# Mixer's step plan: two tiles a step behind each scan, and the shared expert's first unit in step 8 of 20

## The reference, cut to what matters

```python
h = layernorm(x) * (1 + ca) + sa
x_shift = (roll(h, -T//2) @ Wts.T) * sigmoid(gate) + h * (1 - sigmoid(gate))
xn = layernorm(x_shift) * ln_w + ln_b
k, v = xn @ Wk.T, xn @ Wv.T                      # 64 wide
wkv = exp(-exp(time_first) * sigmoid(k)) * v
states = scan(s * exp(time_decay) + wkv_t)       # along the tokens
x = x + ga * (states @ Wo.T)
h = layernorm(x) * (1 + cb) + sb
shared = (silu(h @ Wsg) * (h @ Wsu)) @ Wsd * sigmoid(h @ Wse)   # 1408 wide
routed = top 4 of 32 experts (352 wide, at most 64 tokens each), weights softmax(h @ Wr)
x = x + gb * (shared + routed)
```

## Time and profile before

| | us |
|---|---|
| median of 3 runs | 720.41 (719.29 to 721.12) |
| profiled execution | 720.49 |
| its span, first to last instruction | 718.70 |
| PE busy in the span | 672.3 (94%) |
| DVE / ACT / POOL busy | 367.4 / 288.9 / 185.1 |

### The profile page before, as it was taken

The page is one execution under the profiler, slowest core; times in us unless marked ns, Lnnn a source line. Parts: engine busy times, 40 slices in busy tenths (PEclk is TensorE's granted clock), DMA queues, the critical chain, the costliest instruction groups (busy, mean ns, idle before and its releaser), DMA issues.

```text
span 718.7 us, 8895 instructions
## 1 busy us (share of the span) xinstructions
PE 672.3 (94%) x3218; PEld 466.0 (65%) x3218; DVE 367.4 (51%) x714; ACT 288.9 (40%) x552; POOL 185.1 (26%) x174
## 2 busy tenths in 40 slices
PE   4798688999998899998999899999999999999997
PEld 3665455767676667886665566666666666667875
DVE  3779677678678877763214223122122243225755
ACT  3445775665656633323225124233232343323231
POOL 1254565645536200001122022222221212120000
PEclk9899978999999999999999999999999999999999
DMA  7670200001232008206777767878899787816311
GB/s 276 232 250 0 76 15 30 15 31 30 74 122 84 15 1 281 85 1 242 266 231 239 257 217 253 263 238 280 271 322 339 239 270 261 284 22 234 117 49 69
DMA packets 50295, 118.27 MB, mean 165 GB/s; under 512 B 6904, under 2 KB 11084, under 8 KB 50252
## 3 DMA queue, kind: packets, MB, share of 16 engines
q1 hardware_dynamic: 45388, 109.31, 43.0%
q0 software_dynamic: 4864, 8.40, 5.4%
HBM read 100.87 MB, written 18.91 MB: 167 GB/s over the span
## 4 chain that ended last, share of the span: by engine, by line
PE 61%; DVE 5%; DMA 3%; ACT 2%; issue 2%; POOL 2%; SPq 0%; DVEq 0%; ACTq 0%; POOLq 0%
PE bank L1686 28%; PE bank L1698 11%; PE bank L1741 11%; PE bank L1758 6%; DMA egu<-in_L_ffn_Wu_dram 2%; PE bank L1729 1%; ACT xsH L860 1%; DMA xg<-h_rows,slot_tok 1%; PE bank L1789 1%; PE bank L1747 1%; DVE xres L1260 1%; DVE prodL L1224 1%; POOL ho L634 1%; DVE prod L1222 1%; POOL xres L642 1%
## 5 line engine op out<-in xcount | busy, mean ns | idle before, releaser
L1686 PE MATMUL bank<-xsH,wguH 128*128 128x512 f32 x352 | 143.8, 408 | 1.7 <-DVE xsL L1214 1.3
L1686 PE MATMUL bank<-xsL,wguH 128*128 128x512 f32 x352 | 138.0, 392 | 0.0
L1686 PE MATMUL bank<-xsH,wguL 128*128 128x512 f32 x352 | 137.7, 391 | 0.0
L1741 PE MATMUL bank<-egu,xeT 128*64 128x352 f32 x512 | 80.9, 469 | 3.3 <-DMA egu<-in_L_ffn_Wu_dram 3.3
L1686 PEld LDWEIGHTS bank<-xsH,wguH 128*128 128x128 f32 x352 | 66.6, 189 | 26.4 <-issue 10.8
L1222 DVE TENSOR_TENSOR prod<-bank,silu 128x512 f32<-128x512 f32 x38 | 26.2, 690 | 110.7 <-PE bank L1686 87.7
L1698 PE MATMUL bank<-wdH,prodH 128*128 128x512 f32 x176 | 73.7, 419 | 6.3 <-DVE prodL L1224 4.1
L692 POOL DMA_INDIRECT expert_sums<-ye,slot_to x32 | 49.2, 1537 | 116.7 <-DMA expert_sums<-ye,slot_to 92.0
L1686 PEld LDWEIGHTS bank<-xsL,wguH 128*128 128x128 f32 x352 | 66.3, 188 | 14.7
L1686 PEld LDWEIGHTS bank<-xsH,wguL 128*128 128x128 f32 x352 | 66.6, 189 | 13.0 <-issue 0.7
L699 POOL DMA_INDIRECT xg<-h_rows,slot_tok x16 | 16.8, 1050 | 221.3 <-ACT ye L899 90.2
(11 more groups left out here) (222 smaller groups left out, 1020.8 us busy)
## 6 DMA issues: line engine op xcount, KB each, us to landing
egu<-in_L_ffn_Wg_dram SPq DMA_DIRECT2D x32, 704.0 KB, 6.2
egu<-in_L_ffn_Wu_dram SPq DMA_DIRECT2D x32, 704.0 KB, 7.7
ed<-in_L_ffn_Wd_dram SPq DMA_DIRECT2D x32, 512.0 KB, 5.2
h2T<-in_L_wmod_dram SPq DMA_DIRECT2D x6, 1024.0 KB, 8.7
ed<-in_L_ffn_Wd_dram SPq DMA_DIRECT2D x32, 192.0 KB, 6.3
h_rows<-ho SPq DMA_DIRECT2D x16, 256.0 KB, 2.0
expert_sums<-ye SPq DMA_DIRECT2D x16, 256.0 KB, 8.9
out_dram<-xres SPq DMA_DIRECT2D x16, 256.0 KB, 2.2
```

The costliest lines, as they stand in the source:

```text
L1686: ins = mm.matmul(bk[:, :], l[f][:, w, c, :], r[:, c, :], start=(k == 0), stop=(k == 3 * C - 1))
L1741: ins = mm.matmul(bk[side, 0:F], xeT[:, c, side], egu[:, e, w, c, :], start=(c == 0), stop=(c == C - 1))
```

## The change: what it does

A group's tiles no longer leave one a step, five steps behind their mixer. The new function `outs(t)` gives the tiles that step t projects: none in the step of the group's scan, two in the step behind it, two in the next, none in the fourth. The router of a group stands in that fourth step (t = 7, 11, 15, 19), the shared expert's first unit begins in step 8, and the loop ends after 20 steps. Every engine's step function uses `outs`. ho gets a fourth buffer with its own semaphore; POOL's `out_rstd` stands behind `mix_rows`; the weight splits of the first part (`split_first`, `first_lo`) stand a step earlier; SPLIT_FIRST names the last step alone, and ROUTER_FIRST and the early `lo_group` of step 17 go.

```diff
-        STEPS = NT + 6
-        FFN_FROM = 10
-        ROUTER_FIRST = (9, 17)
-
-        SPLIT_FIRST = (17, 21)
+        STEPS = NT + GT
+        FFN_FROM = 2 * GT
+
+        SPLIT_FIRST = (STEPS - 1,)
+
+        def outs(t):
+
+            g, k = divmod(t - GT, GT)
+            return range(g * GT + 2 * (k - 1), g * GT + 2 * k) if 0 <= g < NG and 0 < k < 3 else ()
...
-            if t >= 6:
-                turns.append(("h2", t - 6))
+            turns += [("h2", i) for i in outs(t - 1)]
...
-            return (t - 9) // GT if t % GT == 1 and t >= 9 else None
+            return t // GT - 1 if t % GT == GT - 1 and t >= GT else None
...
-            PRODUCTS += [("router", router_group(t))] if t in ROUTER_FIRST else []
-            PRODUCTS += [("project", t - 5)] if 0 <= t - 5 < NT else []
+            PRODUCTS += [("project", i) for i in outs(t)]
...
@@ POOL's step loop @@
-                    if 0 <= t - 5 < NT:
-                        out_rstd(t - 5)
...
                     if t + 1 < NT:
                         mix_rows(t + 1)
-                    if t >= 7:
-                        scale_sum(t - 7)
-                        h2_rows(t - 7)
+                    for i in outs(t):
+                        out_rstd(i)
+                    for i in outs(t - 2):
+                        scale_sum(i)
+                        h2_rows(i)
...
-                scale_sum(NT - 1)
-                h2_rows(NT - 1)
+                for i in outs(STEPS - 2):
+                    scale_sum(i)
+                    h2_rows(i)
...
@@ ACT's step loop @@
-                    if t in ROUTER_FIRST:
-                        logits_out(router_group(t))
-                    if 0 <= t - 5 < NT:
-                        norm_out(t - 5)
+                    for i in outs(t):
+                        norm_out(i)
...
-                    if 4 <= t < 4 + NC0 + 1:
-                        split_first(t - 4)
+                    if 3 <= t < 3 + NC0 + 1:
+                        split_first(t - 3)
...
@@ DVE's step loop @@
-                    if t == 17:
-                        lo_group(0, g + 1)
...
-                    if 0 <= t - 5 < NT:
-                        residual_sum(t - 5)
+                    for i in outs(t):
+                        residual_sum(i)
...
-                    if t >= 7:
-                        scale_rows(t - 7)
+                    for i in outs(t - 2):
+                        scale_rows(i)
...
-                scale_rows(NT - 1)
+                for i in outs(STEPS - 2):
+                    scale_rows(i)
...
@@ PE's step loop @@
-                    new_states = t == 13
-                    if 0 <= t - 5 < NT and not new_states and t not in ROUTER_FIRST:
-                        project(t - 5)
+                    new_states = t % GT == 1
+                    for i in () if new_states else outs(t):
+                        project(i)
...
                     if g >= 0:
                         early_piece(g, 2 * s)
-                    if 0 <= t - 5 < NT and new_states:
-                        project(t - 5)
+                    for i in outs(t) if new_states else ():
+                        project(i)
...
-                    if t in ROUTER_FIRST:
-                        project(t - 5)
```

More of the change, by code:

```diff
@@ L79, in build @@
     R = E + 2
+    HO = 4
     assert (H, S, C, CAP * 2, BT, NP, FS % P, HB, PARTS[0]) == (512, 64, 4, P, 8, 16, 0, GT, 2)
@@ L138, in build @@
             mx = sb("mx", [P, 3, H], F32, pa)
-            ho = sb("ho", [P, 3, H], F32, pa)
+            ho = sb("ho", [P, HO, H], F32, pa)
             kvW = sb("kvW", [P, C, P], F32, pa)
@@ L256, in build @@
          xhat_ok, hi_ok, lo_ok, wr_zero, s_full0, s_full1, s_taken0, s_taken1, mix_ok,
-         xn_ok, ho_ok, h2_ok, h2_sent0, h2_sent1, h2_sent2, e_tanh, e_fac, st_ok,
+         xn_ok, ho_ok, h2_ok, h2_sent0, h2_sent1, h2_sent2, h2_sent3, e_tanh, e_fac, st_ok,
          vef_ok, vex_ok, veh_ok, rsf_ok, rsx_ok, rsh_ok, dve_self, pool_self,
@@ L263, in build @@
              "xhat_ok hi_ok lo_ok wr_zero s_full0 s_full1 s_taken0 s_taken1 mix_ok "
-             "xn_ok ho_ok h2_ok h2_sent0 h2_sent1 h2_sent2 e_tanh e_fac st_ok "
+             "xn_ok ho_ok h2_ok h2_sent0 h2_sent1 h2_sent2 h2_sent3 e_tanh e_fac st_ok "
              "vef_ok vex_ok veh_ok rsf_ok rsx_ok rsh_ok dve_self pool_self "
@@ L281, in build @@
         stage_in = (stage_in0, stage_in1, stage_in2)
-        h2_sent = (h2_sent0, h2_sent1, h2_sent2)
+        h2_sent = (h2_sent0, h2_sent1, h2_sent2, h2_sent3)
         d_full, d_used, y_in = (d_full0, d_full1), (d_used0, d_used1), (y_in0, y_in1, y_in2, y_in3, y_in4)
@@ L348, in build @@
             PRODUCTS += [("mixer", t)] if t < NT else []
-            PRODUCTS += [("router", router_group(t))] if t in ROUTER_FIRST else []
-            PRODUCTS += [("project", t - 5)] if 0 <= t - 5 < NT else []
+            PRODUCTS += [("project", i) for i in outs(t)]
             PRODUCTS += [("kv", scan_group(t))] if scan_group(t) is not None else []
-            PRODUCTS += [("router", router_group(t))] if t not in ROUTER_FIRST and router_group(t) is not None else []
+            PRODUCTS += [("router", router_group(t))] if router_group(t) is not None else []
         turn_at, turns_in = {}, dict.fromkeys(T_BANKS, 0)
@@ L511, in _ @@
                     sp.wait_ge(h2_ok, t + 1)
-                    sp.dma_start(h2_dram[t * P:(t + 1) * P, :], ho[:, t % 3, :]).then_inc(h2_sent[t % 3], 16)
+                    sp.dma_start(h2_dram[t * P:(t + 1) * P, :], ho[:, t % HO, :]).then_inc(h2_sent[t % HO], 16)
                     if t == BT - 2:
@@ L534, in load_down @@
                         sp.dma_start(ed[0:F - 2 * P, e, 2, :], Wd[2 * j + e, 2 * P:F, :]).then_inc(dn_in, 16)
-                for k in range(3):
-                    sp.wait_ge(h2_sent[k], 16 * len(range(k, NT, 3)))
+                for k in range(HO):
+                    sp.wait_ge(h2_sent[k], 16 * len(range(k, NT, HO)))
                 sp.wait_ge(wlo_ok, splits(2, 0))
@@ L633, in h2_rows @@
                         pool.wait_ge(sb_in, 16 * (b + 1))
-                    gp.tensor_tensor(ho[:, t % 3, :], ho[:, t % 3, :], bc[:, PLACE[K_SB], :], ALU.add).then_inc(h2_ok, 1)
+                    gp.tensor_tensor(ho[:, t % HO, :], ho[:, t % HO, :], bc[:, PLACE[K_SB], :], ALU.add).then_inc(h2_ok, 1)
                 def scale_sum(t):
@@ L783, in norm_out @@
                         act.wait_ge(part_full, len(VECTORS))
-                    else:
-                        act.wait_ge(h2_sent[t % 3], 16 * (t // 3))
+                    elif t >= HO:
+                        act.wait_ge(h2_sent[t % HO], 16 * (t // HO))
                     act.wait_ge(nbh_ok, t + 1)
-                    a.activation(ho[:, t % 3, :], xres[:, t, :], ACT.Identity, scale=rsh[:, at], bias=nbh[:, at]).then_inc(hn_ok, 1)
+                    a.activation(ho[:, t % HO, :], xres[:, t, :], ACT.Identity, scale=rsh[:, at], bias=nbh[:, at]).then_inc(hn_ok, 1)
                 def part_out(n):
@@ L986, in _ @@
                     if router_group(t) is not None:
-                        if t not in ROUTER_FIRST:
-                            logits_out(router_group(t))
+                        logits_out(router_group(t))
                         sigma_exp(router_group(t))
@@ L1178, in scale_rows @@
                     turn_full(dve, ("h2", t))
-                    v.tensor_tensor(ho[:, t % 3, :], ho[:, t % 3, :], bc[:, PLACE[K_1CB], :], ALU.mult).then_inc(ho_ok, 1)
+                    v.tensor_tensor(ho[:, t % HO, :], ho[:, t % HO, :], bc[:, PLACE[K_1CB], :], ALU.mult).then_inc(ho_ok, 1)
                 def kv_scan(g):
@@ L1437, in _ @@
                             first_rows(i)
-                    if t >= 7:
-                        scale_rows(t - 7)
+                    for i in outs(t - 2):
+                        scale_rows(i)
                     if g >= 0 and s == 3:
                         top_experts(g)
-                    if 6 <= t < 6 + NC0 + 1:
-                        first_lo(t - 6)
+                    if 5 <= t < 5 + NC0 + 1:
+                        first_lo(t - 5)
                     if t == 4:
@@ L1458, in _ @@
                         derive_gb()
-                    if router_group(t) is not None and t != 17:
+                    if router_group(t) is not None:
                         lo_group(0, g + 1)
-                scale_rows(NT - 1)
+                for i in outs(STEPS - 2):
+                    scale_rows(i)
                 down(0, EARLY - 1, 2)
@@ L1467, in _ @@
                 mixer_over(dve)
-                for k in range(3):
-                    dve.wait_ge(h2_sent[k], 16 * len(range(k, NT, 3)))
+                for k in range(HO):
+                    dve.wait_ge(h2_sent[k], 16 * len(range(k, NT, HO)))
                 for u, (p, g) in enumerate(UNITS):
@@ L1583, in turn @@
                             pe.wait_ge(hn_ok, t[1] + 1)
-                            r = ho[:, t[1] % 3, :]
```

(1 more changed line is left out.)

## The result

The median went from 719.85 us (717.33 to 721.12) to **754.68 us** (748.43 to 755.92): ratio 1.0471 (1.0436 to 1.0505), slower by 34.8 us. The forecast was 728.0, the upper end of its range 734. The sign was right, the size was not.

The account below looks back on a forecast made before the run. PE was taken to bound everything after the front, a loop over other engines the front. Lead -5.2, replaced idle and slow time -5.8, new waits +15.75, behind the plan +2.7: +7.5, so 728.0 us; range 717.5 to 734.

Parts of the forecast that it names:

- slow 1.7 in the same stretch, replaced: Main stretch: the 1.7 us that the kernel before loses on PE at a lower granted clock was subtracted from the sum.
- the lead: Front, steps 5 to 8: the first shared-expert unit starts earlier, net of PE work still undone; 5.2 us, bounds 2.2 and 9.5.
- the three named waits: Signs: PE waits before projections of tiles 7 and 11 for mx, before h2(6) for hT, before the third unit for xsL.
- project(7): Step 10: PE's projection of tile 7 waits for mix_front of its own step, 1.6 us.
- h2(6): Step 11: PE's turn of tile 6 waits until ACT has copied h(12) and DVE lowered it, 3.05 us.
- (b): Steps 10 and 14: project(7) and project(11) wait for mix_front of their own step, 1.6 and 1.7 us.
- (c): Turns alternating over two banks: step 11's h2(6) waits 3.05 us and step 15's h2(11) 1.85, plus 0.8 for second h2 turns.
- "heavier" rival: The front gets no earlier as PE returns at the lower clock: lead 2.2, slower lower products in (b); 734, chance 0.10.
- Behind the plan: Between last router and fourth unit: two rows are left behind the loop on DVE and POOL, 2.7 us, bounds 0 and 4.
- the time of 731: Alternative total if each table switch also drained some 1380 ns, making the chain of (b) 1.4 later in two groups.
- The gain: Rival: ACT keeps up, without (b) and the 4.9 of (c), and with a lead of 9.5; 715.5 us, chance 0.15.
- the cancelled terms: Rival: lead 9.5 with half of the new waits, or present lead without (b) and (c); say 720 us, chance 0.15.

Follow-up runs that it names:

- e5: Kernel before with one added PE wait in step 13, ahead of the router's first half, until ACT has normalised tile 8: 728.12 us, 1.0101.
- e8: e5 with 18 unread filler matmuls of 512 columns put ahead of its added wait: 725.16 us, 1.0065.
- e2: Changed kernel with 39 unread filler matmuls ahead of five PE waits (two projections, two h2 turns, the third unit): 747.19 us, 1.0377.
- e1: Kernel before with four added PE waits behind mixers, in steps 11, 12, 14 and 15, until that step's mix_front has read the bank: 736.67 us, 1.0258.
- e3: Changed kernel with POOL's out_rstd ahead of mix_rows again: 743.26 us, 1.0314.
- e11: e9 plus both last scale_sums ahead of the last h2_rows on POOL and 14 filler matmuls ahead of turns h2(6) and h2(11): 730.35 us, 1.0162.
- e9: Changed kernel reordered: out_rstd before mix_rows, step 15's split before logits, second projection behind unit piece in half the projecting steps, ACT's next rows earlier: 733.48 us, 1.0175.

## Why the prediction was wrong, point by point

- **The step that failed: PE's clock.** The sum priced the new waits at their own length and put the clock behind them at nothing; it even took 1.7 us off as "slow 1.7 in the same stretch, replaced". Only a rival of chance 0.10 had a clock price, 3 us, and that for the front. The clock measured +14.1. Of the 25.8 us by which the sum missed, this term is 15.8, the waits 4.7, the lead 2.8. The prediction had both halves in hand: it placed 15.75 us of new waits, and it read from the earlier trace rows that PE fell to a mean of 0.86 where it was busy 51 of 62 us. It did not join them. e5 and e8 show the link with one wait in before, e2 at the places that its filler covered in the changed kernel.

  Its signs of being right mostly came, and would have misled: the first half unit ended at 109.62 (107 +- 3 was said), hT(8) stands at 92.03 (near 91), the three named waits are there, and PE stands idle well over 8 us. None of these looks at the clock. The last router product, 260.69 for a forecast near 237, shows the miss.

  The Trainium skill, "TensorE: Matmul & The Clock Gate", section "HAM oscillation — how this bites in real kernels", describes a kernel whose waits for DMA bring the lower clock back again and again. The trace agrees in kind, with waits for other engines (0.68 in 146.90 to 168.50, around the wait of 5.36 us); e1 adds that 11.8 us of waits may also cost only some 4.
- **The waits** were found at their places, with these sizes (predicted, measured): project(7) 1.6, 2.24; project(11) 1.7, 2.38; keys and values 0.75 each, 0.83, 0.83 and 0.78; h2(11) 1.85, 1.79; third unit 1.8, 2.02; third down product 1.7, 1.75; the second h2 turns 0.8 in all, 0.5; the router's second half 0.95, 0.29 (at the turn ahead of it); **h2(6) 3.05, 5.36**; project(5) none, 1.16. The 2.31 us by which h2(6) was off stand as one row in ACT's timeline, and POOL's timeline has the cause:

```profile
148.07 0.86 ACT L766 ACTIVATE xhat<-xres,nb,rs 128x512 f32<-128x512 f32 x1
...
152.28 0.29 ACT L780 ACTIVATE nbh<-negh,rsh 128x1 f32<-128x1 f32 x1 [2.31 <-POOL rsh L609]
...
154.59 1.28 ACT L833 ACT_TABLE_LOAD   x1
155.88 0.31 ACT L833 ACTIVATE logits<-logits 128x128 f32<-128x128 f32 x1
156.09 0.58 ACT L741 ACTIVATE hT<-bank 128x512 fp32r<-128x512 f32 x1
```

```profile
149.07 1.29 POOL L626 TENSOR_TENSOR mx<-xhat,bc 128x512 f32<-128x512 f32 x1 [9.14 <-ACT xhat L766]
150.44 1.29 POOL L630 TENSOR_TENSOR mx<-mx,bc 128x512 f32<-128x512 f32 x1
151.69 1.07 POOL L609 TENSOR_TENSOR rsh<-veh,neg_half 128x1 f32<-128x1 f32 x2
```

  mix_rows(11) waits for ACT's next row, which stands behind eight h2T copies; out_rstd, put behind mix_rows by the change, waits with it, and ACT then waits for out_rstd. The prediction put rsh behind mix_rows in the front and in (b), but left POOL out of the chain of (c), which this wait belongs to. It forgot that an operation moved behind another also inherits that one's wait. e3, with the old order, measured 2.93, near the 3.05 of the prediction.
- **The lead** was 2.4, at the lower bound of 2.2, and for the reason given there: the router and mixer(8) ran in a stretch with a granted clock of 0.60 (mixer(8) 5.1 us, 101.73 to 106.86, and not 2.95; the router 6.88 us for its 32 matmuls, where the full level gives twice 1.87). That was the "heavier" rival's first half.
- **Behind the plan**: 2.7 predicted, 3.3 measured; e11's order of the two scale_sums gave some 1.3 back.
- **Table loads**: six more, as counted (ACT 558 instructions for 552). The Exp began 0.01 us behind the load's end (155.88 for 154.59 and 1.28), so no drain is in the rows. The Trainium skill, "ScalarE: Activation LUTs", section "What ACT_TABLE_LOAD costs", gives one of some 1380 ns; the trace does not agree, and the time of 731 by it finds no support here.
- **The gain, the cancelled terms**: not borne out. The gain left 7.6 of the 15.75 us of new waits, the cancelled case 10.8 or 7.6; PE waited 20.5.

## What to carry to other kernels

Where a change adds waits to the engine that bounds the stage, price each twice: the wait, and the work behind it at the lower clock. The second price goes by the place: 4.28 us among turns and narrow products came with 5.7 us more in e5's profile, 11.8 us ahead of projections with some 4 in e1, and 1.79 us at h2(11) with none. When an operation is put behind another in a queue, take over what that other one waits for, not only its duration. A plan moved to another phase has to be followed in each engine's queue, for each step of the period: here most of the loss came back by order alone (21 of 35 us in e9).

## What the runs showed of the hardware that was not expected

Unread work in the place of a wait can be nearly free: in e8 18 matmuls of 512 columns, 4.36 us, stand where e5 waits 4.28 us, and PE's other work takes 103.3 us and not 108.87. That e8 is also faster as a whole (725.16 for 728.12 us) is not clear of noise, each beside its own before.

The granted clock does not follow the length of the waits alone: 11.8 us of added waits ahead of projections left it at 0.96 (e1), one of 4.28 us ahead of a router brought it to 0.93 (e5). In the changed kernel 1.16 us ahead of project(5) is followed by matmuls 0.43 us apart, 1.79 us at h2(11) by none, and at h2(6) 2.93 us (e3) and 5.36 us are both followed by a half router of 3.46 to 3.47 us. Which property of a place decides (the narrow products, the turns, or their order) was not separated.
